# Cross-attention and FFN with LoRA on one core: one load of the parameters, A_eff in f32 with half of it ahead of block 0, the column term as a matmul, the first W maxima moved

## What is computed

```python
def fake_quant(x, scale, zp):
    q = jnp.clip(jnp.round(x / s + z), 0.0, 255.0)
    return (q - z) * s
x = x + jnp.matmul(fake_quant(_layernorm(x), s1, z1), fake_quant(ctx, s2, z2))
y = _layernorm(x)
A_eff = jnp.einsum('bn,nri->bri', gate, lora_A)       # 8 gates, 16 LoRAs, rank 32
B_eff = jnp.einsum('bn,nor->bor', gate, lora_B)
x = x + y @ W + bias + B_eff(A_eff y) + B_shared(A_shared y)
```

## Time and profile before

| | us |
|---|---|
| median of 3 runs | 1163.47 |
| the profiled execution, its own time | 1165.81 |
| its span, first to last instruction | 1164.2 |
| PE busy (matmuls) | 1013.1 |
| DVE, ACT, POOL busy | 599.5, 323.7, 247.6 |
| mean granted clock of PE | 0.943 |

### The profile page before, as it was taken

One profiled execution on the slowest core, in us unless ns is written; L12 is line 12 of the kernel. 1 busy time (PEld: TensorE's weight loads), 2 busy tenths in 40 slices (PEclk: granted clock), 3 DMA queues, 4 the chain that ended last, 5 costly groups with the idle time before them and its releaser, 6 DMA issues.

```text
span 1164.2 us, 12162 instructions
## 1 busy us (share of the span) xinstructions
PE 1013.1 (87%) x4663; PEld 475.3 (41%) x4663; DVE 599.5 (51%) x786; ACT 323.7 (28%) x303; POOL 247.6 (21%) x246
## 2 busy tenths in 40 slices
PE   0388795778968999899999599998999999999995
PEld 0138342233525444344444244444554444444442
DVE  4952775898754546456441567798745114014010
ACT  1872545332210213213211244442213003003000
POOL 1030303351000130140150044440110301301200
PEclk9895797898988999999999799999999999999998
DMA  8872275545664731741759843356683305204010
GB/s 344 246 212 73 73 278 237 150 126 159 131 155 147 260 137 68 248 180 69 233 205 282 251 160 137 134 118 164 136 216 120 125 24 163 76 31 149 9 45 18
DMA packets 131736, 177.24 MB, mean 152 GB/s; under 512 B 104816, under 2 KB 104816, under 8 KB 119408
## 3 DMA queue, kind: packets, MB, share of 16 engines
q1 hardware_dynamic: 102000, 117.99, 34.3%
q0 software_dynamic: 11904, 50.34, 12.4%
q10 hardware_dynamic: 17792, 8.39, 2.9%
HBM read 124.26 MB, written 27.26 MB: 130 GB/s over the span
## 4 chain that ended last, share of the span: by engine, by line
PE 47%; DVE 22%; DMA 9%; ACT 8%; issue 8%; POOL 2%; ACTq 1%; SPq 1%; DVEq 0%; POOLq 0%
PE psum L961 13%; PE psum L962 13%; PE psum L963 13%; DVE stage L1159 4%; DVE ring L1163 3%; ACT x L767 3%; PE psum L984 3%; PE psum L889 2%; DMA xn<-in_x 2%; DMA stage<-in_w 2%; DVE x L1202 2%; DMA bias_sb<-in_bias 2%; POOL x L494 2%; DVE stats L1119 2%; ACT stage L617 2%
## 5 line engine op out<-in xcount | busy, mean ns | idle before, releaser
L961 PE MATMUL psum<-ring,lhs 128*128 128x512 f16 x1024 | 389.9, 381 | 21.8 <-DMA lhs<-hl 16.6
L962 PE MATMUL psum<-ring,lhs 128*128 128x512 f16 x1024 | 389.8, 381 | 0.0
L963 PE MATMUL psum<-ring,lhs 128*128 128x512 f16 x1024 | 389.5, 380 | 0.0
L841 PE MATMUL psum<-ring,lhs 128*128 128x512 bf16 x1024 | 236.0, 392 | 67.9 <-DVE ring L1163 57.1
L841 PEld LDWEIGHTS psum<-ring,lhs 128*128 128x128 bf16 x1024 | 101.6, 100 | 199.2 <-DVE ring L1163 60.8
L961 PEld LDWEIGHTS psum<-ring,lhs 128*128 128x128 f16 x1024 | 100.5, 98 | 145.3 <-issue 19.5
L963 PEld LDWEIGHTS psum<-ring,lhs 128*128 128x128 f16 x1024 | 100.6, 98 | 121.9 <-issue 1.9
L962 PEld LDWEIGHTS psum<-ring,lhs 128*128 128x128 f16 x1024 | 100.5, 98 | 120.4 <-issue 1.4
L1233 DVE SCALAR_TENSOR_TENSOR x<-psum,sc,x 128x512 f32<-128x512 f32 (+1 forms) x64 | 45.4, 747 | 182.3 <-PE psum L973 181.4
L494 POOL TENSOR_TENSOR x<-x,bias_sb 128x512 f32<-128x512 f32 (+1 forms) x64 | 88.5, 1407 | 216.0 <-DVE xn L1220 139.3
L624 ACT ACTIVATE ring<-stage,sc 128x2048 f16<-128x2048 f32 x32 | 63.6, 2000 | 214.1 <-PE psum L963 161.2
(11 more groups left out here) (128 smaller groups left out, 708.8 us busy)
## 6 DMA issues: line engine op xcount, KB each, us to landing
stage<-in_w SPq DMA_DIRECT2D x40, 1024.0 KB, 6.2
stage<-in_ctx_in SPq DMA_DIRECT2D x32, 1024.0 KB, 4.9
out<-x POOLq DMA_DIRECT2D x64, 256.0 KB, 3.6
x<-in_x POOLq DMA_DIRECT2D x8, 1024.0 KB, 14.9
xn<-in_x POOLq DMA_DIRECT2D x8, 1024.0 KB, 7.5
x<-in_x POOLq DMA_DIRECT2D x4, 2048.0 KB, 13.1
lhs<-in_lora_a SPq DMA_DIRECT2D x4, 1024.0 KB, 6.5
lhs<-in_lora_b SPq DMA_DIRECT2D x4, 1024.0 KB, 8.1
```

Of the source, the lines that this page charges most:

```text
L841: last = pe.matmul(psum[:, t, :], lhs_q[:, k, t * P:(t + 1) * P], ring_q[:, g, j % 2, u, :], start=(k == 0), stop=(k == KT - 1))
L961: pe.matmul(psum[:, t, :], hi, ring[:, g, 0, u, :], start=(kk == 0), stop=False)
L962: pe.matmul(psum[:, t, :], hi, ring[:, g, 1, u, :], start=False, stop=False)
L963: last = pe.matmul(psum[:, t, :], lo, ring[:, g, 0, u, :], start=False, stop=False)
```

## The change

- The four scalars and the gates come in one array, by one load (`par`).
- The centre is 127 instead of 128. The column sum is made of ones scaled by 32, evicted by ACT as f16 and its rest by DVE (`column_low`, lower 64 partitions); one matmul a tile with `ones` adds it into the tile's bank (`column_term`), after tile 3 for tiles 0 to 3 (in the first block after tile 4 for 0 to 4). The column sum has bank 7 in every block. `adjust` on POOL is gone. `psum_full` is now given by that matmul, and `evict1` waits for it and for the row term.
- A_eff: quarters 0 and 1 are made ahead of block 0 (`a_effective(0)`, `(1)`, copied by DVE), 2 and 3 after it, followed at once by all of B_eff (eight steps, each of two matmuls into one bank of 128 partitions). A_eff is stored in f32; the gates of a batch are loaded back (`load_gates`) and scaled and split during its block 1 (`shared_hi`, `gate_hi`, `shared_low`, `gate_low`).
- Context groups 2 and 3 of block 0 of each batch have buffers of their own (`load_head`, `conv_head`, `head_group_mid`, `head_group_end`).
- W's four maxima for block 0 are taken from LoRA's buffers after blocks 1 and 2 (`max_of_first_w`); in phase 2 the two loads for block 1's maxima stand behind `turn_y(b, 4)`.
- `turn_next` goes from ACT's to SP's queue; x is quantised through three buffers; row terms of blocks 1 to 3 of batch 0 are one pass per tile.

```diff
-CENTRE = 128.0
+CENTRE = 127.0
+ONES = 2.0 ** 5
+COL_SCALE = 2.0 ** -16
...
-            sp.dma_start(gate_p, gate).then_inc(gate_in, 16)
-            for c, v in ((S1, s1), (Z1, z1), (S2, s2), (Z2, z2)):
-                sp.dma_start(c, v.rearrange("(a n) -> a n", a=1).to_broadcast([P, 1])).then_inc(par_in, 16)
+            sp.dma_start(pats_sb[:, 0:4 + NGATE], par).then_inc(par_in, 16)
...
+            def load_head(b, g):
+
+                sp.dma_start(head_buf(b, g), ctx_v[b, 0, g].rearrange("p (h u) n -> p h (u n)", h=2)).then_inc(head_in[g - 2], 16)
+
             def load_lora_a(c):
-                sp.dma_start(lora_in_slot(c), lora_a[c]).then_inc(la_in[c], 16)
+                if c >= 2:
+                    sp.wait_ge(pa_full, (c - 1) * KC)
+                sp.dma_start(la_slot(c), lora_a[c]).then_inc(la_in[c], 16)
             def load_lora_b(c):
-                sp.wait_ge(pa_full, (c + 1) * (KT // NBLK))
-                sp.dma_start(lora_in_slot(c), lora_b[c]).then_inc(lb_in[c], 16)
+
+                if c < 2:
+                    sp.wait_ge(q_rows, TILES)
+                else:
+                    sp.wait_ge(pa_full, (c + 1) * KC)
+                sp.dma_start(lb_slot(c), lora_b[c]).then_inc(lb_in[c], 16)
+
+            def load_gates(b):
+
+                if b == 0:
+                    for n in range(2):
+                        sp.wait_ge(ag_dram[n], 16 * (NBLK // 2))
+                    sp.wait_ge(be_full, 2)
+                else:
+                    sp.wait_ge(base_done, NBLK * TILES)
+                    sp.dma_start(ash(b), lora_as).then_inc(sh_again, 16)
+                sp.dma_start(a_gates, ag_scratch[:, b * GPB:(b + 1) * GPB, :, :]).then_inc(ag_in, 16)
+
...
             sp.wait_ge(x_in[1], 16)
-            load_ctx(0, 0, [0, 1])
+            load_ctx(0, 0, [0])
+            load_lora_a(0)
+            load_ctx(0, 0, [1])
+            load_head(0, 2)
+            load_lora_a(1)
+            load_head(0, 3)
             turn_q(0)
             turn_q(1)
-            load_ctx(0, 0, [2, 3])
+            load_lora_a(2)
+            sp.dma_start(ash(0), lora_as).then_inc(sh_in, 16)
             turn_q(2)
             turn_q(3)
-            sp.dma_start(ash, lora_as).then_inc(sh_in, 16)
-            load_lora_a(0)
-            load_lora_a(1)
+            load_lora_a(3)
+            turn_q(4)
+            turn_q(5)
             load_ctx(0, 1, [0, 1])
-            for t in range(4, TILES):
-                turn_q(t)
-            load_lora_a(2)
-            load_lora_a(3)
+            turn_q(6)
+            turn_q(7)
+            load_lora_b(0)
+            load_lora_b(1)
             load_ctx(0, 1, [2, 3])
-            load_ctx(0, 2, range(NG))
+            load_lora_b(2)
+            load_lora_b(3)
             sp.wait_ge(sh_in, 16)
+            sp.wait_ge(csum_full, 1)
             sp.dma_start(bsh, lora_bs.rearrange("r (a o) -> (r a) o", a=P // RANK)).then_inc(sh_in, 16)
-            for c in (0, 1, 3):
-                load_lora_b(c)
+            load_ctx(0, 2, [0, 1])
+            load_gates(0)
+            load_ctx(0, 2, [2, 3])
+            load_first_w(0)
+            load_first_w(1)
             load_ctx(0, 3, range(NG))
-            for n in range(2):
-                sp.wait_ge(a_dram[n], 16 * (NGATE // 2))
-            load_lora_b(2)
+            load_first_w(2)
+            load_first_w(3)
+
...
-                    load_ctx(b, 0, range(NG))
+                    load_ctx(b, 0, [0, 1])
+                    sp.wait_ge(q_rows, (b + 1) * TILES)
+                    load_head(b, 2)
+                    for t in range(2):
+                        sp.wait_ge(turned[t], turns1(b, t) - 16)
+                    load_head(b, 3)
+                    for t in range(TILES):
+                        turn_next(b, t)
+                    load_gates(b)
                     with sp.Fori(1, NBLK) as j:
-                        ctx_block(b, j, grp1(b, 0, 0), j * NG + grp1(b, 0, 0))
-                else:
-                    w_peaks_block(0)
+                        ctx_block(b, j, grp1(b, 0, 0), j * NG + (grp1(b, 0, 0) - 2))
...
                 turn_y(b, 4)
+                if b == 0:
+                    w_peaks_block(1)
                 load_a(b, 2)
                 turn_y(b, 5)
-                if b == 0:
-                    w_peaks_block(1)
...
-                    adjust(0, 0)
-                    adjust(0, 1)
+                    store_a_part(2)
+                    store_a_part(3)
                     largest(1, MX_A, PW_A)
-                    for g in range(NGATE):
-                        pool.wait_ge(a_lo, g + 2)
-                        pool.dma_start(a_scratch[g], a_f16[:, g % 2, :, :]).then_inc(a_dram[g % 2], 16)
-                    adjust(0, 2)
                     for c in range(NBLK):
-                        pool.wait_ge(be_out, (c + 1) * NQ)
-                        pool.dma_start(bg_rows[:, :, c * NW:(c + 1) * NW], b_buf[c % 2]).then_inc(bg_dram[c % 2], 16)
-                    adjust(0, 3)
+                        pool.wait_ge(be_out, 2 * (c + 1))
+                        pool.dma_start(bg_rows[:, :, c * NW:(c + 1) * NW],
+                                       b_part[c % 2].rearrange("p (q o) -> p q o", q=NQ // 2)).then_inc(bg_dram[c % 2], 16)
                     largest(2, MX_B, PW_B)
+                    store_a(b)
                     largest(3, MX_W, PW_W)
                 else:
                     load_residual(b, NBLK - 1)
-                    for j in range(NBLK):
-                        adjust(b, j)
+                    store_a(b)
...
             act.wait_ge(consts, 1)
             root_pair(0)
             relu_rows(0)
             relu_rows(1)
+            ctx_block(0, 0, [0])
+            root_pair(1)
             ident_rows(0)
             ident_rows(1)
-            root_pair(1)
-            ctx_block(0, 0, [0])
             relu_rows(2)
+            relu_rows(3)
             ctx_block(0, 0, [1])
-            relu_rows(3)
             ident_rows(2)
             ident_rows(3)
-            ctx_block(0, 0, [2])
+            conv_head(0, 2)
+            conv_head(0, 3)
             root_pair(2)
-            ctx_block(0, 0, [3])
             relu_rows(4)
             relu_rows(5)
             ident_rows(4)
...
+                act.wait_ge(rows_ready, b + 1)
+                if b == 0:
+                    ctx_block(b, 1, [0, 1])
+                    row_terms(0, 1)
+                    column(0)
+                    ctx_block(b, 1, [2])
+                    for k in range(2 * KC, 3 * KC):
+                        a_eff_out(k)
+                    ctx_block(b, 1, [3])
+                    for k in range(3 * KC, KT):
+                        a_eff_out(k)
+                    for n in range(8):
+                        b_eff_out(n)
+                    row_terms(1, NBLK)
+                else:
+                    ctx_block(b, 1, [0])
+                    column(0)
+                    ctx_block(b, 1, [1])
+                    act.wait_ge(res_in[0], 16)
+                    row_terms(0, 1)
+                    ctx_block(b, 1, [2, 3])
+                for j in range(1, NBLK):
+                    if j < NBLK - 1:
+                        ctx_block(b, j + 1, [0])
+                    column(j)
+                    if j < NBLK - 1:
+                        ctx_block(b, j + 1, [1])
...
+            def column_term(b, j, tiles):
+
+                n = b * NBLK + j
+                pe.wait_ge(col_ready, n + 1)
+                for t in tiles:
+                    pe.matmul(psum[:, t, :], ones[:, :], col_parts[:, n % 2, :], start=False, stop=True).then_inc(psum_full, 1)
...
                 half = TILES // 2
+                a_effective(0)
+                a_effective(1)
                 for g in range(NG):
-                    pe.wait_ge(converted, grp1(0, 0, g) + 1)
+                    ring_ready(0, 0, g)
                     for t in range(half):
                         if g == 0:
                             tile_start(0, 0, t)
                         group1(0, t, g)
-                first_column_sum()
+                column_sum(0, 0)
                 for t in range(half, TILES):
                     tile_start(0, 0, t)
                     for g in range(NG):
                         group1(0, t, g)
+                    column_term(0, 0, range(half + 1) if t == half else [t])
+                a_effective(2)
+                a_effective(3)
+                for n in range(8):
+                    b_effective(n)
...
+                    if t == (0 if j else 2):
                         column_sum(b, j)
+                    if t >= TILES // 2 - 1:
+                        column_term(b, j, range(t + 1) if t == TILES // 2 - 1 else [t])
...
+            def column_low(b, j):
+
+                n = b * NBLK + j
+                v = col_parts[P // 2:P, n % 2, :]
+                dve.wait_ge(col_hi, n + 1)
```

(58 more changed lines are left out.)

519 lines of the change are left out of this document (295 added, 224 removed).

## The result

| | before | after |
|---|---|---|
| median of the runs | 1163.33 us (1159.76 to 1165.22, 4 runs) | 1120.53 us (1119.00 to 1122.65, 4 runs) |
| profiled execution, span | 1165.8, 1164.2 us | 1122.65, 1121.1 us |
| mean granted clock | 0.943 | 0.973 |

After / before is 0.9637, 95% interval 0.9608 to 0.9665: the changed kernel is faster, by 42.8 us. By spans (first to last instruction of the profiled execution) 43.1 us were gained where the sum had 30.5.

What follows compares the result with a forecast made beforehand. PE, busy 87% of the span, was taken as the bound, with gains in its gaps and in work that need not be PE's. 18 + 10.5 + 2 = 30.5 us off 1165.8 gives 1135.3, or 1133 against the median; range 1110 to 1151.

Steps and rivals of the forecast that it cites:

- the sum: Whole kernel: 18 us to the first FFN, 10.5 in batch 0's FFN, 2 in batch 1; 30.5 gained.
- (a): Blocks 0, 1 and batch 1: column waits do not bind, 28 us less, about 1106; 0.14 including what lies below 1125.
- the column waits: PE waits for the column term: 19 us in block 0, 7 in block 1, 5 in batch 1.
- The bounds: Margins on the stages, -7, -4, +3, +2 and 2 us in each wait, giving 1125 to 1142.
- (b): A part gives nothing: moved maxima loads (10.5) or A_eff's early half (14); 1143 to 1150; 0.17 together with (d).
- the head start: Start: one parameter load lets statistics run some 7 us earlier, a gain that does not reach PE.
- the six loads: Start: loads of 1.05 MB each ahead of the first transpose; PE's main pass starts 3 us later.
- the lower bound: A_eff's second half, costed at 13.8 us: at full clock 3 to 7 us less.
- the moved loads: FFN of batch 0: W loads for maxima issued earlier, PE's 13.5 us wait falls to 3, 10.5 gained.
- (c): Phase 1, every block: column wait trips the clock, slower kernel, taken as 1170 us; chance 0.06.
- (d): Start: A_eff's early half is not early, LoRA A load 1 landing last; only 7 us move; 0.17 together with (b).

Runs made afterwards that it cites:

- parameters late: The changed kernel with VectorE's start held until x tile 2 has landed too: 1121.40 us, ratio 0.9613.
- transposes first: The changed kernel with the loads of LoRA A 1 and head 3 issued behind transposes 0 and 1: 1117.40 us, ratio 0.9577.
- The last kernel: Changed kernel plus two loads behind transposes, earlier tail column terms, B_eff stores first, early column sums, split row terms, reordered copies and context loads: 1090.45 us, ratio 0.9379.
- the one with the two edits that gained: Changed kernel with LoRA A 1 and head 3 behind transposes 0 and 1, last blocks' column terms from tile 1: 1108.29 us, ratio 0.9529.

## Why the prediction was right, and where its sizes were off

The range held, though not for the reason that it was drawn for. What lies below 1125 was given 0.14, with rival (a), in which the column waits don't bind. They did bind, and the time came under 1125 by the clock of A_eff and by smaller terms. That the range reached there was in part luck. The bounds were also added up too narrowly: -7 and -4 alone reach 1122. Two other sums are off: 1133 less 28 is 1105, and (b) with both its parts (24.5) gives 1157, beyond the range that was to take all of it.

In spans: 43.1 us gained, forecast 30.5. By stage (us gained; a minus is a loss):

| stage | forecast | measured |
|---|---|---|
| to the FFN's start, batch 0 | 18 | 24.3 (266.62 to 242.31) |
| FFN of batch 0 | 10.5 | 11.7 |
| batch 1, phase 1 | 2 | 4.1 |
| FFN of batch 1 and end | 0 | 3.0 |

One execution of a kernel is not exact to a microsecond. The kernel before, profiled again, starts the FFN of batch 0 at 266.71 as before, but its FFN of batch 0 is some 3 us shorter (batch 1 starts at 648.4 and not 651.5); so the second row of the table is known to about 3 us. No run undoes the joining of B_eff to A_eff, the heads' own buffers or the move of `turn_next`; what they gave is read from the timelines alone.

**Start.** The main pass was to start at 55.5 and did at 54.6. That the head start wouldn't reach PE is shown (parameters late), and that the six loads hold the transposes is too (transposes first). What the forecast missed is that this order was worth 5 to 7 us: it priced the queue and did not ask what another order would give.

**Block 0.** Eighth tile at 85, measured 82.4; column wait from 76.4 to 95.5, measured from 73.6 to 93.1 (19 us and 19.5); end at 109.5, measured 107.1. The chain behind it is as written, two context Relus, eight row terms, column, low half:

```profile
82.71 4.08 ACT L696 ACTIVATE stage<-stage,pats_sb,sc 128x2048 f32<-128x2048 f32 x2 [0.36 <-DVE sc L1272]
86.70 4.99 ACT L850 ACTIVATE x<-x,sc 128x512 f32<-128x512 f32 x8
91.59 0.67 ACT L844 ACTIVATE bias_sb<-psum,sc 128x512 f16<-128x512 f32 x1
```

**A_eff.** Here the largest error of the sum lies. The term was mis-sized: 13.8 us forecast, 7.25 measured. The forecast took the half clock of the row before with the lower bound beside it (3 to 7 less), and the lower bound came true to the full. The half clock was taken as given for these matmuls, while what PE had done ahead of them decided it. Here 14 us of dense matmuls stood ahead of it, the last 10 at full clock, with no wait between. That reading was open from the trace of before: its A_eff came behind 7.92 us of idle time. The Trainium skill (TensorE: Matmul & The Clock Gate, HAM oscillation — how this bites in real kernels) puts the loss of the clock down to long idle gaps. The 4.58 us gap agrees. The 1.08 us wait within A_eff doesn't: it is no long gap, and cost the clock all the same.

**B_eff and block 1.** B_eff took 15.2 us, not 14; its 1.22 us wait is the difference. Block 1 lost 3.6 to the forecast: the wait for the B_eff stores, costed at 0 to 3, was 4.8 (137.82), the one for the column 4.6 where 7 were forecast, and each brought some 3.5 us of half clock. Block 2 and the tail each came out about 1 us better (39.4 from block start to FFN where I had 40.2). In sum, to the FFN's start: 2.4 + 6.5 - 1.2 - 3.6 + 2.0 = 6.1 of the 6.3 us more.

**FFN of batch 0.** The wait fell to 3.1 (forecast 3), and the moved loads are shown to be the cause (11.8 us more when moved back).

**Batch 1.** Block 0 gained 8.5 us, as forecast: it takes 36.9 (615.55 to 652.48), with a 4.5 us column wait where I had 5. Two periods of 29.57 gained 0.48 each, where I had 0.3. The tail lost 5.3 and not 6.8.

**End.** 2.7 us in what follows the last matmul: not forecast, and not explained.

**Rivals.** (a) did not come: the column waits bind. Its price of 28 us for their absence was wrong as well: taken away alone they were worth 2.5. The last kernel, which has none of them, is 17.8 faster than the one with the two edits that gained, but it has other edits too. (b) is excluded for both parts that it named: the maxima's loads were worth 11.8, and the early half of A_eff 13.5 by medians (8.8 by ratio), though it does hold block 0 back by 4.9. (c) did not come: the five blocks for which no column wait was forecast have none. Block 2 of batch 0 takes 30.8 us, with a 1.1 us wait for an eviction, and full blocks behind it 29.6 at full clock. (d) did not come: A_eff's second quarter was done at 45.0, and PE then still waited 3.9 us for transpose 2.

## What to carry to other kernels

A clock read beside an operation belongs first to what stood ahead of it. When a change moves weak work (small matmuls) behind dense work, cost it at both clocks, and see to it that nothing makes it wait within, since here the small matmuls did not win the clock back in 23.6 us. In one queue, what the first consumer needs goes ahead of what has room: two loads moved behind two transposes gave the 5 us that they take to move, and 2 more. And when a wait is removed alone, look at each engine's next item in order; here three waits of 28.6 us in all gave 2.5 when taken away alone, and 17.8 more came only with the work behind them reordered on several engines.
